# Mixer's last turns and the dispatch in one stage: dispatch begun behind the last but one pair's outputs, only the last pair solved in halves

## The reference

```python
def _L0_attn_ref(...):               # gated delta rule, 16 heads of 64
    mixed = silu(causal_conv(hidden @ W_qkv.T)); z = hidden @ W_z.T
    def step(Sst, inp):              # over the 114 tokens
        Sst = Sst * exp(g_t); kv = einsum(Sst, k_t)
        delta = (v_t - kv) * b_t
        Sst = Sst + k_t * delta; o = einsum(Sst, q_t)
    h_ = o * silu(z); h_ = h_ * rsqrt(mean(h_ * h_) + EPS) * norm_weight
    return h_ @ W_out.T
def _L0_ffn_ref(...):                # E = 32 experts, K = 4, C = 256 places each
    logits = x @ gate_w.T; topk_w, topk_idx = top_k(softmax(logits), K)
    slot = place of each choice in its expert, tokens in order; over C is dropped
    buf[e_s, slot] = x[t_s]          # the dispatch
    routed = experts(buf), gathered back with the weights
    shared = silu_and_mul(x @ shared_w_gate_up) @ shared_w_down
    return routed + shared
h = h + _L0_attn_ref(_layernorm(h), ...)
h = h + _L0_ffn_ref(_layernorm(h), ...)
```

## Time and profile before

| | us |
|---|---|
| median of 3 runs | 2871.31 (2869.2 to 2872.5) |
| span of the profiled execution, first to last instruction | 2864.9 |
| median less that span | 6.4 |
| mixer's last three iterations and the stage's end | about 1846 to 2004 of the span |
| dispatch | 2004 to 2220 |

### The profile page before, as it was taken

The page is one execution under the profiler, slowest core; times in us unless marked ns, Lnnn a source line. Parts: engine busy times, 40 slices in busy tenths (PEclk is TensorE's granted clock), DMA queues, the critical chain, the costliest instruction groups (busy, mean ns, idle before and its releaser), DMA issues. The chain is left out here.

```text
span 2864.9 us, 53688 instructions
## 1 busy us (share of the span) xinstructions
PE 2380.9 (83%) x19286; PEld 1823.1 (64%) x19286; DVE 2012.3 (70%) x4812; ACT 1292.8 (45%) x3118; POOL 851.1 (30%) x708
## 2 busy tenths in 40 slices
PE   7999998996468989898989898777552948899798
PEld 6777777885446777676767677555431845577454
DVE  4888884334468888888888888952663447896673
ACT  1444442111457777676767777743000314444132
POOL 2111100001023333333333333331577037650110
PEclk9999998996679999999999999988665978899799
DMA  4210001003102222222222222221211952210000
GB/s 152 88 59 29 13 7 56 22 25 121 64 20 49 53 52 53 54 53 54 53 54 53 53 53 52 49 68 35 88 37 19 295 174 74 57 47 1 24 22 27
DMA packets 274342, 168.97 MB, mean 59 GB/s; under 512 B 182847, under 2 KB 250318, under 8 KB 273728
## 3 DMA queue, kind: packets, MB, share of 16 engines
q1 hardware_dynamic: 247949, 140.28, 17.3%
q0 software_dynamic: 26112, 25.03, 3.3%
HBM read 99.23 MB, written 73.45 MB: 60 GB/s over the span
## 5 line engine op out<-in xcount | busy, mean ns | idle before, releaser
L1333 POOL TENSOR_TENSOR qd<-decay,qm 114x456 f32<-114x456 f32 x128 | 163.7, 1299 | 551.0 <-DVE qm L1448 467.0
L1838 PEld LDWEIGHTS d_ps<-d_xT,resid 128*128 128x128 f32 x1024 | 197.1, 194 | 46.1 <-issue 29.0
L1838 PE MATMUL d_ps<-d_xT,resid 128*128 128x228 f32 x1024 | 215.7, 363 | 12.3 <-DMA d_xT<-normed_t 12.3
L1429 DVE TENSOR_TENSOR ue<-ue,elim_tmp 128x30 f32<-128x30 f32 (+14 forms) x480 | 211.9, 441 | 16.8
L2578 POOL DMA_INDIRECT s_eo<-rows_y,slots_all x128 | 154.3, 1206 | 146.5 <-POOLq L2390 108.5
L1491 DVE SCALAR_TENSOR_TENSOR y_v<-raw,taps,y_v 128x228 f32<-128x228 f32 x384 | 164.4, 500 | 47.4 <-ACT y_v L1643 47.4
L1427 DVE TENSOR_TENSOR elim_tmp<-ue 128x30 f32<-128x30 f32 (+14 forms) x480 | 179.1, 373 | 25.2 <-issue 9.8
L1605 ACT ACTIVATE decay<-d_ps,gates 114x114 f32<-114x114 f32 x512 | 138.0, 362 | 85.0 <-DVE nt L1461 50.9
L1491 DVE SCALAR_TENSOR_TENSOR y_qk<-raw,taps,y_qk 128x228 f32<-128x228 f32 x384 | 145.0, 452 | 23.6 <-ACT y_qk L1643 23.6
L2142 POOL DMA_INDIRECT rows_x<-r_xn,slot x128 | 144.1, 1126 | 52.4 <-issue 50.6
L1616 ACT ACTIVATE gl<-upto,gates 114x114 f32<-114x114 f32 x512 | 156.1, 393 | 0.4
(11 more groups left out here) (343 smaller groups left out, 5559.7 us busy)
## 6 DMA issues: line engine op xcount, KB each, us to landing
rows_x<-zero_row SPq DMA_DIRECT2D x4, 2048.0 KB
ue<-blocks_n SPq DMA_DIRECT2D x16, 512.0 KB, 5.0
blocks_u<-ue SPq DMA_DIRECT2D x16, 512.0 KB, 2.8
blocks_v<-on SPq DMA_DIRECT2D x16, 512.0 KB, 2.9
e_x<-rows_x SPq DMA_DIRECT2D x32, 256.0 KB, 4.5
e_gu<-L_ffn_w_gate_up SPq DMA_DIRECT2D x32, 256.0 KB, 4.4
rows_y<-e_y SPq DMA_DIRECT2D x32, 256.0 KB, 3.4
blocks_n<-nt SPq DMA_DIRECT2D x96, 64.0 KB
```

What stands on the lines that cost most here:

```text
L1333: pool.tensor_tensor(qd[p.par][s][:, hs(u), :].rearrange("p (a o b) t -> p a o b t", o=2, b=2)[:, :, o], e[o][:, :, :].rearrange("p (a b) ...
L1429: step = dve.tensor_tensor(ue[:, 0:j, j + 1:], ue[:, 0:j, j + 1:], part, ALU.subtract)
L1838: last = pe.matmul(ps[:, f % 2, (t % 2) * W:(t % 2 + 1) * W], w_qkv[:, k, t * 128:(t + 1) * 128], xT[:, k, :], start=(k == 0), stop=(k == ...
```

## The change

The stage `route` is gone; its steps stand in `delta_net`, in the orders of the last turns that each engine now has written out.

- The dispatch's first two groups are normalised on DVE inside iteration 15, between pair 14's gates and its outputs; their powers stand on POOL ahead of `clear_gap`. From then on each engine's order mixes dispatch steps with the solving and putting out of pair 15: groups 0 to 5 among them, groups 6 and 7 (samples of the last pairs) behind the last output.
- Only the last pair is solved in halves: chains 0 and 1 (sample 0) to their outputs, then chains 2 and 3, in banks 0, 1, 6 and 7; banks 2 to 5 go to the dispatch. `vbank`, `xbank` and `strand` pick banks and counts by `r.last`.
- The shared expert's `gate_up`, `shared` and `down` of all groups stand behind the last pair's output products.
- The dispatch's large tiles lie in tiles of the mixer that are free by then (`raw`, `y_qk`, `y_v`, `nt`, `qd`); there are four normalised groups and five turned ones instead of three and one. The mixer's weights move up by one slot of the arena, so that groups of rows can be loaded when a weight has been read for the last time; groups 0 to 3 are loaded ahead of iteration 15, `w_gate` at the stage's start.

```diff
-    VBANK, XBANK = (4, 5, 0, 1), (6, 7, 2, 3)
...
+        def vbank(r, m):
+            return m % 2 if r.last else (4, 5, 0, 1)[m]
+        def xbank(r, m):
+            return 6 + m % 2 if r.last else (6, 7, 2, 3)[m]
+        def strand(r, q, m):
+            return 4 * (m // 2) + 2 * q + m % 2 if r.last else 4 * q + m
...
+                def load_rows(g):
+                    if g >= GROUPS - 2:
+                        for s in range(2):
+                            sp.wait_ge(h_out[s], 16 * (2 * g + 2))
...
+                def last_turns():
+                    iteration(Pair(0, 14))
+                    sp.wait_ge(qkv_mm, PAIRS * 8)
+                    for g in range(EARLY):
+                        load_rows(g)
+                    iteration(Pair(0, 15), proj=False)
...
+                    iteration(Pair(0, 16), a=False, proj=False)
+                    sp.wait_ge(z_mm, 4 * PAIRS)
+                    load_rows(4)
+                    load_rows(5)
+                    iteration(Pair(0, 17), a=False, proj=False, z=False)
+                    sp.wait_ge(wo_mm, 2 * PAIRS)
+                    load_rows(6)
+                    load_rows(7)
...
             @block.gpsimd
...
+                    query_decay(p, 7)
+                    power(0)
+                    power(1)
+                    pool.wait_ge(rrstd, 2)
+                    clear_gap(r, p, done, True, True, 8, 2, 2)
...
+                    scatter(0, 0)
+                    power(2)
...
+                    scatter(1, 0)
+                    power(3)
...
+                    clear_gap_of(r, 0)
+                    scatter(2, 0)
+                    pool.wait_ge(x_gap, r.n * 2 + 1)
+                    power(4)
...
+                    clear_gap_of(r, 1)
+                    pool.wait_ge(x_gap, r.n * 2 + 2)
+                    scatter(3, 0)
+                    power(5)
...
+                    done = Pair(0, 15)
+                    gate_power(done, 0)
+                    gate_scale(done, 0)
+                    gate_power(done, 1)
+                    gate_scale(done, 1)
+                    for s in range(GS):
+                        scatter(4, s)
+                    power(6)
+                    scatter(5, 0)
+                    scatter(5, 1)
+                    power(7)
...
             @block.vector
+                    choose(0)
+                    gate_mean(done, 0)
+                    gate_mean(done, 1)
+                    eliminate(r, 1, 9)
+                    place(0)
+                    statistics(2)
+                    choose(1)
+                    eliminate(r, 9, 18)
+                    place(1)
+                    normalise(2)
+                    share(0)
+                    gate_silu(r, 0)
+                    residual(done, 0)
+                    eliminate(r, 18, 31)
+                    turn_inverse(r)
+                    statistics(3)
+                    choose(2)
+                    gate_silu(r, 1)
...
+                    residual(done, 1)
+                    shared(0)
+                    add_shared(0)
+                    shared(1)
+                    statistics(6)
...
             @block.tensor
+                    outputs(r, 0)
+                    outputs(r, 1)
+                    counts(3)
+                    turn(4)
+                    gate_logits(4)
+                    join(r, 2, False)
+                    join(r, 3, False)
...
+                    turn(5)
+                    gate_up(0)
+                    gate_logits(5)
+                    counts(5)
+                    output_turn(done, 0)
+                    output_product(done, 0)
+                    output_turn(done, 1)
+                    output_product(done, 1)
+                    down(0)
+                    gate_up(1)
```

More of the change, by code:

```diff
@@ L2365, in experts @@
+                first_turns(iteration)
+                with pe.Fori(0, LOOPS) as j:
+                    for k in range(2):
+                        iteration(Pair(j, 4 + k))
+                last_turns()
 def experts(c, rows_x, rows_y):
```

792 lines of the change are left out of this document (493 added, 299 removed).

## The result

The changed kernel took 2824.11 us (median of 4 runs, 2818.35 to 2827.15) where the kernel before took 2871.15: the ratio is 0.9831, interval 0.9811 to 0.9851, a gain of 47.0 us. The forecast was 2816, with 2792 to 2848 as its range. Its profiled execution took 2827.15, with a span of 2824.2.

What follows compares the result with a forecast made beforehand. POOL's queue of 128 scatters was taken to bound the dispatch: 1943.0 + 188.8 + 11.2 + stalls 12 + stretch 4 + tail 2 = 2161.0. Next stage 2165.6 instead of 2220.4, gain 54.8: 2816 us, range 2792 to 2848.

Steps and rivals of the forecast that it cites:

- Where the scatters start: Start of the dispatch: first scatter at 1943.0, 84 us earlier, with pair 14 late by 4.4 us.
- POOL decides: At the first scatter: POOL's pair 14 gates end at 1941.6, after place(0) gives its slots at 1940.7.
- The stretch of POOL beside DVE: Gate operations of both pairs meet DVE's work: 4 us in all added to POOL's time.
- POOL's queue: POOL's dispatch work: scatters with powers 188.8 us, plus pair 15's gate operations and two gap memsets 11.2 us.
- the rivals in which every scatter is held by DVE or elimination by scatters: Scatters held by DVE: no change or slower, chance 0.07; elimination waiting for scatters: 2862 us, chance 0.04.
- (1): POOL's wait at power(3), behind 20 scatters, for statistics(3) on DVE: stall 2 us.
- (3): POOL's wait at power(6) for statistics(6), so for the last pair's output: 1 to 12 us, taken as 5.
- (4): POOL's wait for slots of groups 6 and 7: a tie, 0 to 5 us, taken as none.
- the worst end: Worst case of the sum: start 4 us later, stalls 23, rest unchanged; gain 39.8 us, time 2832.
- Wait (2): POOL's wait at the second gap memset for join(15, 3): 3.5 to 9 us, taken as 5.
- The tail: End of the dispatch: shared expert's last groups end at 2157 to 2168, POOL at 2155; 2 us added.
- The rival that PE's lower clock lets the shared expert end the stage: End of the dispatch: PE and the shared expert end it, 2832 to 2860 us, likeliest 2841; chance 0.18.

Runs made afterwards that it cites:

- The last version: Against the reordered version with pair 15's gate_scale on DVE: place(0) ahead of eight elimination steps, counts(0) ahead of output_turn(14, 0); 2792.18 us, ratio 0.9727 to the kernel before.
- power(3) later: Against the changed kernel, power(3) on POOL moved from behind scatter(1, 0) to behind scatter(1, 3); 2826.67 us, ratio 0.9856 to the kernel before.
- the three reordered ones: Changed kernel with its whole order rearranged, 2795.09 us; that with pair 15's gate_scale on DVE, 2800.17; the latter with place(0) and counts(0) earlier, 2792.18.

## Why the prediction was nearly right, and what was mis-sized

The forecast is 8 us off the median and inside its range, but the stretch came that near by errors that cancel in part: 16 us too little in some terms of the sum, 6.4 too much in others.

**Where the scatters start** (52.3 forecast, 55.7 measured). The delay of pair 14 by the two powers was right in place and size: 4.0 for 4.4. Its price was too low, 4.4 in the sum where the edit that takes it out gained 9.3: behind the idle time in front of the substitute PE's granted clock was 0.89 and not 1.00, which cost 1.65 us, and the chain to the second joins got longer. The step that failed is "POOL decides". POOL's gates ended at 1939.62, but place(0) gave its slots only at 1942.43: one elimination step took 1.87 us, beside the gate_scale at 1930.99, and one tensor_scalar of place(0) 2.53, beside the gate_scale at 1936.83 and the memset behind it. The last version shows it: with place(0) earlier POOL does decide. (The prediction's own terms for the slots, 5.0 + 4.35 behind a second gate_mean that ends at 1930.8, add up to 1940.2 and not 1940.7, which would not have changed its choice.)

**The stretch of POOL beside DVE** (4 forecast in POOL's queue, none measured there). The victim was wrong, and that the size came out is luck, since the forecast spread it over the gates of both pairs. In the changed kernel it is DVE that waits beside pair 14's gates, 1.6 us longer in the elimination step and 2.3 in place(0) than the 0.3 and 0.2 that such operations took elsewhere, and it shows at the first scatter. The forecast had it as the worst case of that start, and in the sum at another place. The Trainium skill (SBUF — State Buffer, "Who interferes with whom") calls the port pair of DVE and GpSimd an exclusive lock; three DVE operations that ended within 0.15 us of the end of a POOL operation over 1024 elements agree with it. So do scatters held by DVE, as the prediction's sentence on turn_inverse's copy had it. In the changed kernel none met that copy, as POOL was waiting at power(3); but in each of the four versions in which one began beside it (power(3) later and the three reordered ones) that scatter took 1.78 to 1.80 us instead of 1.12, so 0.7 for the 1 of the prediction. In the two versions with gate_scale on DVE three more, beside its products, took 1.45 to 2.06.

**POOL's queue** (188.8 + 11.2 forecast, 189.4 + 10.8 measured) was right, and with it the fall of the rivals in which every scatter is held by DVE or elimination by scatters: single scatters are held, not all 80.

**The waits** were right in their places, and (1) and (3) nearly in their sizes: 3.1 for 2, 5.9 for 5. (4) was taken at nothing and measured 3.9, within its bounds of 0 to 5; the worst end, with 23 us of waits, left these 5 out. In the other versions that keep the tail's order (4) was 0.8 to 2.5, with logits(6) at 1.78, and not there without the shared expert. Wait (2), forecast 3.5 to 9, was taken at 5 and measured 9.3, and it is the term of the sum that was most mis-sized: the joins it waits for ended 16.9 us behind the first half's outputs, where the sum had 14, or 16.5 with PE rows of the lower level. That alternative was what came: turn(4) 1.78, logits(4) 3.30. I chose the quicker one although PE had stood idle ahead of both. The outputs themselves ended 5 to 8 us later than forecast (123.4 behind the gate_silu), but POOL came to the memset 5.4 later too. Adding the waits up is sound as an account of POOL's time, as the table does; it says nothing of what one is worth. They hang on one chain, and (1) and (2) taken out alone gave 1.8 and 1.4 us, no more than scatter(7, 0) waited less (3.1 and 1.4).

**The tail** was forecast as 2 us behind POOL. The last add ended at 2165.10, 1.3 ahead of POOL's last scatter: a tie, which the text of the prediction foretold within 10 us. The rival that PE's lower clock lets the shared expert end the stage (likeliest 2841) did not come, with gate_up at 3.22 in four of eight groups (4.3 to 6.1 in the others) and down at 1.98 in five, but without the shared expert 8.2 us go, through POOL's waits at power(6) and scatter(7, 0).

## What to carry to other kernels

Where two stages are merged so that one engine's queue never dries, list its waits as ends of chains, not as terms of a sum: a wait cut out alone comes back at the next place where that queue needs the late chain. Here three edits that took out single waits of 3 to 9 us (the third took out two) gave 1.4 to 2.6, and the reordering of the whole chain 26, of which one edit, the earlier clear_gap, gives 9.3 alone. An operation moved in front of a short one that another engine needs (two powers of 1 us in front of a memset of 0.5) can cost more than its length when PE falls idle by it: 4.0 us of delay, 9.3 in the stretch.

## What was not expected of the hardware

Many of PE's rows behind 3 us and more of idle time stood at the lower level, 1.2 GHz, and came back to 2.4 GHz only some rows later: 1.94 and 1.12 us for the same sixteen matmuls, 3.30 and 1.78 for logits. Filling 10 of 13 us of a wait with matmuls raised the mean granted clock of the wait to 0.90 and left the rows directly behind its last 2.7 idle us at the lower level. gate_product(3) took 1.97 in five versions and 3.3 to 3.8 in the others, though it stands behind 2.6 to 3.9 us of idle time in all: what separates them was not settled.
